# Weighted values and their sums of weights as 64-row by 32-column tiles per head

## The reference, cut to what matters

```python
qkv = einsum('bmd,ed->bme', xn, Wqkv)             # 16 heads of 16
k4, v4 = every 8th row of a segment of 512         # 64 keys per segment and head
scores = einsum('bhspd,bhskd->bhspk', q4, k4)      # 512 x 64
c = max(scores over each block of 64 queries)
w = exp(scores - c)
den = sum(w, axis=-1) + 1e-10
num = einsum('bhsnmk,bhskd->bhsnmd', w, v4)
attn = (num / den) @ Wout.T
ffn = relu(xn @ W1 + b1) @ W2 + b2                 # 256 -> 1024 -> 256
out = x + attn + ffn
```

## Time and profile before

| what | value |
|---|---|
| median of 3 runs | 1187.57 us (1187.46 to 1188.78) |
| profiled execution, span | 1189.4 us |
| TensorE busy | 1162.9 us, 98% |
| VectorE busy | 885.6 us, 74% |
| ScalarE busy | 657.1 us, 55% |
| GpSimd busy | 613.5 us, 52% |
| mean granted TensorE clock | 0.993 of 2.4 GHz |

### The profile page before, as it was taken

How to read it: one execution, slowest core, us unless ns; L and a number is a source line. 1 busy time by engine, 2 the same in 40 slices (tenths; PEclk the granted TensorE clock), 3 DMA queues, 4 the chain that set the end, 5 groups by cost and what they waited for, 6 DMA issues and landing times.

```text
span 1189.4 us, 22871 instructions
## 1 busy us (share of the span) xinstructions
PE 1162.9 (98%) x7457; PEld 955.7 (80%) x7457; DVE 885.6 (74%) x1437; ACT 657.1 (55%) x1142; POOL 613.5 (52%) x488
## 2 busy tenths in 40 slices
PE   5799999999999999999999999999999999999998
PEld 3578888888878888888888888888888888888888
DVE  7788777778787777777777787777877777777762
ACT  4545555565655565555565555556555555555653
POOL 2435654465554455554556544556544556544554
PEclk9889999999999999999999999999999999999999
DMA  5423343222333322333222433223343233332210
GB/s 184 99 73 93 85 106 100 63 82 70 101 101 84 80 72 81 98 106 84 68 81 75 106 101 84 72 70 88 101 106 82 56 87 84 106 102 55 67 49 36
DMA packets 75402, 102.24 MB, mean 86 GB/s; under 512 B 13808, under 2 KB 42096, under 8 KB 75376
## 3 DMA queue, kind: packets, MB, share of 16 engines
q1 hardware_dynamic: 75376, 101.90, 32.6%
HBM read 22.16 MB, written 16.78 MB: 33 GB/s over the span
## 4 chain that ended last, share of the span: by engine, by line
PE 96%; DVE 1%; issue 0%; SPq 0%; POOL 0%; DMA 0%; ACT 0%; DVEq 0%; POOLq 0%
PE y_bank L690 39%; PE h_bank L690 38%; PE misc L811 5%; PE s_bank L742 5%; PE misc L814 5%; PE misc L756 2%; PE misc L690 2%; PE misc L781 0%; PE misc L764 0%; DMA q_pack<-q_hi 0%; PE s_bank L690 0%; DVE w_exp L589 0%; DVE s_max L583 0%; DVE xn_keys L544 0%; DVE w_lo L506 0%
## 5 line engine op out<-in xcount | busy, mean ns | idle before, releaser
L338 POOL TENSOR_TENSOR h_lo<-h_full,h_hi 128x512 fp32r<-128x512 f32 x256 | 336.7, 1318 | 557.2 <-ACT h_full L403 553.3
L409 ACT ACTIVATE w_exp<-w_exp 128x512 f32<-128x512 f32 x256 | 162.7, 636 | 238.7 <-DVE w_exp L589 238.7
L690 PE MATMUL y_bank<-w_hi,h_hi 128*128 128x256 f32 x1024 | 290.6, 284 | 0.0
L690 PE MATMUL y_bank<-w_lo,h_hi 128*128 128x256 f32 x1024 | 290.5, 284 | 0.0
L690 PE MATMUL y_bank<-w_hi,h_lo 128*128 128x256 f32 x1024 | 290.2, 283 | 0.0
L596 DVE RECIPROCAL den<-den 128x256 f32<-128x256 f32 x128 | 222.3, 1739 | 39.9 <-ACT den L422 39.9
L401 ACT ACTIVATE h_hi<-h_bank,b_cols 128x512 fp32r<-128x512 f32 x256 | 176.1, 688 | 82.6 <-PE h_bank L690 76.8
L690 PE MATMUL h_bank<-xt_hi,w_hi 128*128 128x512 f32 x512 | 210.8, 412 | 1.9 <-DVE q_lo L611 1.9
L690 PEld LDWEIGHTS y_bank<-w_lo,h_hi 128*128 128x128 f32 x1024 | 196.0, 191 | 9.9
L690 PEld LDWEIGHTS y_bank<-w_hi,h_hi 128*128 128x128 f32 x1024 | 195.5, 191 | 9.3
L690 PE MATMUL h_bank<-xt_lo,w_hi 128*128 128x512 f32 x512 | 201.9, 394 | 0.0
(11 more groups left out here) (91 smaller groups left out, 1708.1 us busy)
## 6 DMA issues: line engine op xcount, KB each, us to landing
q_pack<-q_hi SPq DMA_DIRECT2D x256, 128.0 KB, 2.4
x_raw<-x SPq DMA_DIRECT2D x32, 512.0 KB, 3.3
q_pack<-q_lo SPq DMA_DIRECT2D x128, 128.0 KB, 2.4
out<-y SPq DMA_DIRECT2D x32, 512.0 KB, 2.9
k_pack<-k_hi SPq DMA_DIRECT2D x256, 32.0 KB, 1.9
k_pack<-k_lo SPq DMA_DIRECT2D x128, 32.0 KB, 1.9
x_keys<-x SPq DMA_DIRECT2D x16, 128.0 KB, 3.0
w_exp<-w SPq DMA_DIRECT2D x2, 1024.0 KB, 8.8
```

What stands on the lines that cost most here:

```text
L338: pool.tensor_tensor(h_part[1][:, i % HBUF], h_full[:, i % HBUF], f32(h_part[0][:, i % HBUF]), ALU.subtract).then_inc(h_lo, 1)
L409: act.activation(w_exp[:, pair], w_exp[:, pair], ACT.Exp).then_inc(w_ready, 1)
L690: mm = pe.matmul(ps, stationary[a], moving[b], start=start and c == 0 and n == 0, stop=stop and c == len(pairs) - 1 and n == 2, skip_group ...
```

## The change

v gets 32 columns for each pair and both row halves, in which columns 2d+a hold the values of head a (in its 64 rows) and the other columns hold ones. `weighted_values` now takes, for each pair, one matmul of 64 rows by 32 columns for each head: head 0's rows go to misc[0], head 1's to misc[1]. A bank thus holds, on interleaved rows, the weighted values and the sums of weights of one head. ScalarE drains both banks with a per-row factor `even` (1 on even rows, 0 on odd), and VectorE adds the other bank by the factor `odd` (`merge_heads`): num is then complete with the two heads interleaved, and den is the sums with neighbouring rows swapped. `guard_den` adds 1e-10, `invert_den` swaps neighbouring rows by a stream shuffle and takes the reciprocal of all 512 columns. The rows of wout are interleaved likewise by four DMAs in place of one. The merges take the place of the reciprocals at the end of the step; both whole reciprocals stand after score tiles 2 and 4. `attention_out` moves to i = 6 and 7, `attention_hi` behind the fifth and sixth exponentials, the copy of v behind the statistics. TensorE's waits for weighted values move ahead: for quad 0 before the last token tile of second_product(7), for quad 1 between the two halves of the second tail product; the latter waits for quad 0's merge, as transpose_x and the key products wait for both merges (`num_merged`), in place of the drains.

At the start, the memsets of head_ones go, one for `odd_t` comes, a second transpose makes it a column, and `odd` and `even` are written from it. v is set to 1.0 where it was 0.0. `second_product` takes the range of token tiles as an argument.

```diff
-        v = sb("v", [P, 2, D], F32)
+        v = sb("v", [P, 2, PAIRS, PW], F32)
...
-                sp.dma_start(wout_raw, wout_t.rearrange("(c p) n -> p c n", p=P)).then_inc(w2_loaded, 16)
+                wout_heads = wout_t.rearrange("(c j a d) n -> c a j d n", c=DH, a=2, d=HD)
+                for c in range(DH):
+                    for a in range(2):
+                        sp.dma_start(wout_raw[a::2, c], wout_heads[c, a]).then_inc(w2_loaded, 16)
...
             def attention_out(s, quad):
-                pool.wait_ge(rden_ready, (s * QUADS + quad + 1) * (RP // QUADS))
-                pool.wait_ge(num_ready, s * QUADS + quad + 1)
+                pool.wait_ge(rden_ready, s * QUADS + quad + 1)
                 pool.wait_ge(att_hi, past((s - 1) * QUADS + quad + 1))
                 pool.tensor_tensor(att[:, quad], num[:, quad], den[:, quad], ALU.mult).then_inc(att_ready, 1)
...
                         hidden_lo(past(s), first[i])
                     if i == 2 and attention:
                         residual(s, par)
-                    if i in (4, 6) and ffn:
-                        attention_out(s, i // 2 - 2)
-                    if i in (5, 7) and ffn:
-                        attention_lo(s, i // 2 - 2, par)
+                    if i in (6, 7) and ffn:
+                        attention_out(s, i - 6)
+                if ffn:
+                    for quad in range(QUADS):
+                        attention_lo(s, quad, par)
                 segment, tail = tail_tiles(s, attention)
...
-                act.copy(num[:, quad], misc[0][:]).then_inc(num_ready, 1)
-                act.add(den[:, quad], misc[1][:], GUARD).then_inc(den_ready, 1)
+                act.wait_ge(masks_made, 6)
+                act.activation(num[:, quad], misc[0], ACT.Copy, scale=even[:]).then_inc(num_den_ready, 1)
+                act.activation(den[:, quad], misc[1], ACT.Copy, scale=even[:]).then_inc(num_den_ready, 1)
...
                         exponential(s, i - LAG)
                     if i in first:
                         hidden(past(s), first[i])
-                    if i == 5 and ffn:
-                        attention_hi(s, 0, par)
                 if norm:
                     transposed_hi(s, par)
                 if NH - 1 in first:
...
                 if attention:
                     exponential(s, PAIRS - 3)
                 if ffn:
+                    attention_hi(s, 0, par)
+                if attention:
+                    exponential(s, PAIRS - 2)
+                if ffn:
                     attention_hi(s, 1, par)
-                if attention:
...
-            def invert_den(s, part):
-                quad, n = part // (RP // QUADS), part % (RP // QUADS)
-                columns = slice(n * SEG * QUADS // RP, (n + 1) * SEG * QUADS // RP)
-                dve.wait_ge(den_ready, s * QUADS + quad + 1)
-                dve.reciprocal(den[:, quad, columns], den[:, quad, columns]).then_inc(rden_ready, 1)
+            def merge_heads(s, quad):
+                n = (s + 1) * QUADS + quad + 1
+                dve.wait_ge(num_den_ready, 2 * n)
+                dve.scalar_tensor_tensor(num[:, quad], misc[1], odd[:], num[:, quad], ALU.mult, ALU.add)
+                dve.scalar_tensor_tensor(den[:, quad], misc[0], odd[:], den[:, quad],
+                                         ALU.mult, ALU.add).then_inc(num_merged, 1)
+            def guard_den(s, quad):
+                dve.wait_ge(num_merged, s * QUADS + quad + 1)
+                dve.tensor_scalar(den[:, quad], den[:, quad], GUARD, None, ALU.add).then_inc(den_guarded, 1)
+            def invert_den(s, quad):
+                dve.stream_shuffle(den[:, quad], den[:, quad], [i ^ 1 for i in range(PW)]).then_inc(den_swapped, 1)
+                dve.wait_ge(den_swapped, s * QUADS + quad + 1)
+                dve.reciprocal(den[:, quad], den[:, quad]).then_inc(rden_ready, 1)
...
+            def pair_values(s, par):
                 dve.wait_ge(kv_ready, s + 3)
                 dve.wait_ge(pv_psum, past((s + 1) * QUADS))
                 for a in range(2):
                     dve.tensor_copy(
-                        v[a * KEYS:(a + 1) * KEYS, par].rearrange("p (n a d) -> p n a d", a=2, d=HD)[:, :, a, :],
+                        v[a * KEYS:(a + 1) * KEYS, par].rearrange("p n (d a) -> p n d a", a=2)[:, :, :, a],
                         kv[par * KEYS:(par + 1) * KEYS, D:].rearrange("p (n a d) -> p n a d", a=2, d=HD)[:, :, a, :]
                     ).then_inc(v_ready, 1)
...
                         mask_k(s)
                     if n == 6 and norm:
                         transposed_lo(s, par)
+                    if n in (2, 4) and ffn:
+                        dve.wait_ge(den_guarded, s * QUADS + n // 2)
                     if attention:
                         shift_scores(s, n)
                     if n == 1 and norm:
                         normalise(s + 2, par)
                     if n == 1 and keys:
                         keys_lo(s)
+                    if n in (1, 3) and ffn:
+                        guard_den(s, n // 2)
                     if n in (2, 4) and ffn:
-                        invert_den(s, RP // QUADS + n // 2 - 1)
+                        invert_den(s, n // 2 - 1)
                 if norm:
                     finish_projections(s, par)
                 if load:
                     statistics(s + 3, 1 - par)
                     statistics_done(s + 3)
-                if attention:
-                    invert_den(s + 1, 0)
+                if norm:
+                    pair_values(s, par)
+                if attention:
+                    merge_heads(s, 0)
                 if load:
                     mean_variance(s + 3, 1 - par)
                 if attention:
-                    invert_den(s + 1, 1)
+                    merge_heads(s, 1)
...
+            def first_product_chunk(i, par, c):
+                return three_products(h_bank[i % 2][:],
+                                      [([w[:, c, i * P:(i + 1) * P] for w in w1s], [x_[:, par, c] for x_ in xt])],
+                                      c == 0, c == DH - 1)
...
-            def weighted_values(s, quad, par, norm):
+            def weighted_values_waits(s, quad, norm):
                 pe.wait_ge(v_ready, (s + 2) * 2)
                 pe.wait_ge(w_ready, (s + 1) * PAIRS + PAIRS - (QUADS - 1 - quad))
...
                 if quad == 0 and norm:
                     pe.wait_ge(xt_lo, (s + 3) * DH)
                 else:
-                    pe.wait_ge(num_ready, (s + 1) * QUADS + quad)
-                    pe.wait_ge(den_ready, (s + 1) * QUADS + quad)
-                pairs = range(quad * PAIRS // QUADS, (quad + 1) * PAIRS // QUADS)
-                for j, pair in enumerate(pairs):
-                    pe.matmul(misc[0][PW * j:PW * (j + 1), :], v[:, 1 - par, PW * pair:PW * (pair + 1)],
-                              w_exp[:, pair], start=True, stop=True)
-                for j, pair in enumerate(pairs):
-                    mm = pe.matmul(misc[1][PW * j:PW * (j + 1), :], head_ones[:], w_exp[:, pair],
-                                   start=True, stop=True)
+                    pe.wait_ge(num_merged, (s + 1) * QUADS + quad)
+            def weighted_values(s, quad, par):
+                for j in range(PAIRS // QUADS):
+                    pair = quad * (PAIRS // QUADS) + j
+                    for a in range(2):
+                        rows = slice(a * KEYS, (a + 1) * KEYS)
+                        mm = pe.matmul(misc[a][PW * j:PW * (j + 1)], v[rows, 1 - par, pair], w_exp[rows, pair],
+                                       start=True, stop=True)
                 mm.then_inc(pv_psum, 1)
             def step(s, par, ffn, attention, norm, load):
...
                     for m in range(DH):
                         queries(s, par, m)
                 if ffn:
-                    second_product(s, NH - 1)
-                if attention:
-                    weighted_values(s, 0, par, norm)
+                    second_product(s, NH - 1, range(T - 1))
+                if attention:
+                    weighted_values_waits(s, 0, norm)
+                if ffn:
+                    second_product(s, NH - 1, range(T - 1, T))
+                if attention:
+                    weighted_values(s, 0, par)
                 segment, tail = tail_tiles(s, attention)
-                for i in tail:
-                    first_product(segment, i, 1 - par if attention else par, norm)
-                if attention:
-                    weighted_values(s, 1, par, norm)
+                if tail:
+                    first_product(segment, tail[0], 1 - par if attention else par, norm)
+                    first_product_waits(segment, tail[1], norm)
+                    first_product_chunk(tail[1], 1 - par if attention else par, 0)
+                if attention:
+                    weighted_values_waits(s, 1, norm)
+                if tail:
```

(48 more changed lines are left out.)

22 lines of the change are left out of this document (12 added, 10 removed).

## The result

| kernel | median, us | runs | ratio to before, 95% interval |
|---|---|---|---|
| before | 1188.17 | 4 | |
| changed | 1342.92 (1333.19 to 1346.12) | 4 | 1.129 (1.125 to 1.133) |

The change makes the kernel 13% slower. The forecast was 1300 with a range of 1218 to 1342; the measured median lies 0.9 us past the upper end, inside the spread of its runs, and outside the 1265 to 1330 that the forecast gave as its own range. The profiled execution of the changed kernel has a span of 1344.3 us and a mean granted clock of 0.951 (0.993 before). The spread of the runs goes with that clock: the fastest, 1333.2 us, was granted 0.960, the slowest, 1346.1 us, 0.951.

The account below looks back on a forecast made before the run. TensorE, 98% busy, bounds the kernel before; VectorE's longer queue then delays it. Steps grow 5.0 us with keys and 2.5 without, 7.5 a pair, 112 over some 15 pairs, added to 1187.57: 1300, range 1218 to 1342.

Parts of the forecast that it names:

- the falling clock: Last rival: TensorE stands twice for 2.7 us with keys, clock falls, 2.5 us a pair, 1338; 0.12 shared with halves in turn.
- TensorE's gain: Weighted-values groups: eight tiles side by side take 0.95 us, saving 0.9 us a quad, 1.8 a step; lower bound zero.
- The guard's stand: First guard, behind xn, waits for GpSimd's x_b: 2.2 us without keys, 2.0 with; bounds 0 and 2.2.
- the free guard: Rival: the guard, having no pointer operand, doesn't wait for GpSimd; 3.4 us more a pair, 1239; chance 0.20.
- VectorE's prices: VectorE's new operations: reciprocals 3.26 us each, shuffles 0.73 with wait, merges 0.63, guards 0.46; 32.1 a step against 26.54.
- k_full: Step with keys: VectorE ends k_full at 22.7 us, for 16.5 before, so the xn transposes start 5.4 us later.
- idle 5 us before the xn transposes: Sign of a right forecast: TensorE idle 5 us a pair before the xn transposes, with k_full as releaser.
- From the transposes to S6: Step with keys: from the xn transposes to score matmul 6's start (S6), 2.26 us.
- Behind W: After the first weighted-values group starts (W): merge at W+4.4 us, including 0.6 for attention_hi, then 4.87 to the step's end.
- VectorE above 85% busy: Sign of a right forecast: VectorE above 85% busy while inside a step.
- faster: Rival: VectorE's queue has room and TensorE's saving shows, 31 steps times 1.8 us, 1131; chance 0.13.
- Halves in turn: Rival: the tiles' row halves take turns, 0.9 us back on both groups, 2.7 us a pair, 1341; 0.12 shared with low clock.

Follow-up runs that it names:

- e4: Kernel before with only TensorE's 64-row by 32-column tiles, no merge, swap, guard or long reciprocal, result not computed: 1136.3 us, ratio 0.956.
- e1: Changed kernel with the 1e-10 added by ScalarE as bias of den's drain, both VectorE guards and their waits gone: 1248.6 us, ratio 1.051.
- e2: Changed kernel with the second reciprocal and its swap moved from behind score tile 4 to behind score tile 5: 1305.1 us, ratio 1.098.
- e11: Changed kernel with the first quad's guard right behind shift 0 in place of behind xn: 1319.2 us, ratio 1.111.
- e7: Changed kernel with eight extra matmuls ahead of the kv wait and the xn transposes, only in steps with keys: 1322.5 us, ratio 1.113.
- e12: e6 with TensorE's first-merge wait moved before the second tail product's last matmul and the kv copy one score tile earlier: 1172.6 us, ratio 0.987.
- e6: Changed kernel with e1, e2, e5 and ScalarE's cast of quad 1 (attention_hi) behind q_hi, all together: 1193.0 us, ratio 1.003.
- e5: Changed kernel with the first merge ahead of the loaded segment's statistics and v's copy on VectorE: 1321.8 us, ratio 1.111.

## Why the prediction was right

The direction and the waits were right: VectorE sets the period, the guard stands behind GpSimd, and TensorE waits for kv, k_full and the first merge. The size was forecast too small, 112 us for 155, and came near the end of the wide range because a rival that had been given little came true beside the forecast, the falling clock.

- *TensorE's gain*, 0.9 us a quad: 0.84 in e4. Right.
- *The guard's stand*, 2.0 and 2.2 us: the first guard of a step lasts 2.29 and 2.62, less 0.42 for its own work 1.9 and 2.2. Right, and without a pointer operand, so the free guard is refuted. e1 shows that guard and stand together are on the path.
- *VectorE's prices*: reciprocal 3.27 from start to start (3.26), swap 0.78 (0.73), merge 0.66 (0.63). Right. The 32.1 us a step is a wrong sum: its own terms, put in place of the old reciprocals in 26.54, give 31.3. Nothing else was built on it.
- *k_full*: forecast for 22.7, it ends at 22.96 (650.76 less 627.80). Right, and e2 shows that order alone takes its wait away. The sign "idle 5 us before the xn transposes" was put wrongly; TensorE stands 2.76 us for kv and 2.61 for k_full, as the last rival says.
- *From the transposes to S6*, taken as 2.26: measured 3.68. This is the term that was mis-sized. In the step without keys S5 to S6 took 5.6 us for 3.93 (4.05 in e11, at the full clock). I had the lower clock as a rival of 0.12 shared, and added none of it to the sum, though the forecast itself made TensorE stand twice for 2.7 us in a step. By the steps of e7 and e11 it costs 1.4 us with keys, and by those of e7 0.3 without: some 25 us in 15 pairs, over half of the 43 between forecast and result.
- *The rest of the 43*: 5 us at the ends, and 0.9 a pair in small terms on VectorE that all came out a little longer. In the step without keys shift 3 ends at 15.7 for 15.3 and the first merge at 33.5 for 32.6.
- *Behind W*: the merge at W+4.1 (4.4), 4.94 to the end of the step (4.87). Near, but the 0.6 us taken for attention_hi does not show: ScalarE stood idle for 1.33 us ahead of the drain. Without it the sum was W+3.8.
- *VectorE above 85% busy*: 86% without keys, but 79% with keys.
- *The rivals*: faster is refuted for this order (1343). Its condition was put at 3.4 us less on VectorE before k_full, which holds with a free guard only; by the sum it is 5.4 (22.7 for 17.3). e12 gets under the kernel before with the guard off VectorE and a new order. Halves in turn is refuted by the 1.09 us group.

Of the 155 us lost, taking the guards off VectorE gives 94 back (e1), 12 of them through the clock; the new order on VectorE and ScalarE gives most of the rest (1249 to 1193 from e1 to e6), again with the clock, which is full for all transposes in the steady steps of e6. The tiles' gain of 52 (e4) was there all along, under it.

## What to carry to other kernels

When work is moved from a busy engine to one that is 75% busy, add up the second engine's whole queue from one end of the period to the other, its unavoidable waits included, before believing the gain; here 6.4 us more on VectorE in each step, its stand included, were to save TensorE 1.7, and a pair of steps became 10 us longer. With the guard moved to ScalarE and the rest placed well, the same tiles brought 1.3%. Check what each added VectorE operation in SBUF meets on GpSimd at that moment, and where TensorE will stand, price its lower clock as well. When a run changes the time more or less than the waits explain, look at each step for that clock before giving the edit the credit: in e5 and e11 it made most of the difference.

## What the runs showed of the hardware

- A tensor_scalar in SBUF with an immediate, started while GpSimd's x_b ran, stood until 0.29 us after its end: 2.29 us beside one of 2.45, 0.42 us alone. Moving it moved the stand to its neighbour (e11).
- Eight fp32 tiles of 64 rows by 32 columns run side by side: 16 instructions in 1.09 us, each 601 ns.
- Behind stands of 1.8 to 2.8 us TensorE's granted clock fell to 0.50 or 0.51 (1.2 GHz) in some steps and not in others: eight transposes took 1.94 us in one step of e11 and 1.07 in another, behind the same two stands. In e1 they took 1.94 behind a single stand of 2.60. In the changed kernel's step without keys they took 1.91 behind one of 1.80. When it falls these runs do not settle. Filling the stands with useless matmuls made the kernel 20 us faster (e7).
- A stream shuffle of 512 columns takes 745 ns, a scalar_tensor_tensor with a PSUM operand and a pointer 742 to 751 ns, a reciprocal of 512 columns 3353 ns.
